# A state-space and feed-forward layer on one core: the same steps in another order on all five engines

## What is computed

```python
x = x + attn(layernorm(x))      # state-space layer, see below
x = x + ffn(layernorm(x))

def attn(u):
    zxbcdt = u @ W_in.T         # z0, x0 (512 each), xBC (544), dt (8 heads)
    dt = softplus(zxbcdt[..., -8:] + dt_bias);  A = -exp(A_log)
    xBC = silu(causal_conv4(xBC) + conv_b)      # x (8 heads x 64), B (16), C (16)
    h = exp(dt_t * A) * h + dt_t * x_t * B_t    # scanned over the rows
    y = h @ C_t + D * x_t
    y = layernorm(y) * ln_gamma + ln_beta
    y = sigmoid(y @ W_gate.T + b_gate) * y
    return concatenate([silu(z0) * x0, y]) @ W_out.T

def ffn(x):
    h = gelu(x @ ternary(W_fc).T)
    return layernorm(h, ln_w, ln_b) @ ternary(W_proj).T
```

## Time and profile before

| | us |
|---|---|
| median of 3 runs | 1097.28 |
| lowest and highest run | 1093.89, 1099.71 |
| span of the profiled execution, first to last instruction | 1095.2 |
| PE busy in it | 1049.7 (96%) |
| DVE busy | 966.7 (88%) |
| ACT busy | 962.1 (88%) |
| POOL busy | 496.6 (45%) |

### The profile page before, as it was taken

The page is one execution under the profiler, slowest core; times in us unless marked ns, Lnnn a source line. Parts: engine busy times, 40 slices in busy tenths (PEclk is TensorE's granted clock), DMA queues, the critical chain, the costliest instruction groups (busy, mean ns, idle before and its releaser), DMA issues.

```text
span 1095.2 us, 23188 instructions
## 1 busy us (share of the span) xinstructions
PE 1049.7 (96%) x8214; PEld 668.4 (61%) x8214; DVE 966.7 (88%) x2007; ACT 962.1 (88%) x1740; POOL 496.6 (45%) x590
## 2 busy tenths in 40 slices
PE   3877999999999999999999999999999999999997
PEld 1543756566575666657565665756666566666674
DVE  5998998999989999988999898899998988788766
ACT  5978698999999988899898999989899997989775
POOL 1543564353534544444434726443263733544552
PEclk9888999999999999999999999999999999999999
DMA  6702434245445265455336564353645433543668
GB/s 199 203 12 39 100 76 78 50 98 116 98 91 95 50 126 98 107 97 96 72 78 116 103 121 87 89 95 62 117 97 113 87 80 63 117 78 64 115 124 161
DMA packets 306708, 105.94 MB, mean 97 GB/s; under 512 B 275488, under 2 KB 302880, under 8 KB 306592
## 3 DMA queue, kind: packets, MB, share of 16 engines
q1 hardware_dynamic: 306592, 104.46, 47.7%
HBM read 24.32 MB, written 8.39 MB: 30 GB/s over the span
## 4 chain that ended last, share of the span: by engine, by line
PE 70%; DVE 11%; ACT 8%; issue 4%; DMA 3%; SPq 2%; POOL 1%; ACTq 0%; DVEq 0%; POOLq 0%
PE bank L399 44%; PE bank L634 8%; PE bank L622 7%; PE bank L560 3%; PE bank L569 2%; PE bank L475 2%; ACT L183 2%; DMA hT<-hb 2%; DVE cv L1018 2%; PE bank L521 1%; DVE EM L1138 1%; DVE st L981 1%; PE bank L545 1%; ACT EM L799 1%; DMA x<-in_x 1%
## 5 line engine op out<-in xcount | busy, mean ns | idle before, releaser
L399 PE MATMUL bank<-xnT,win 128*128 128x512 f16 (+1 forms) x1248 | 299.5, 387 | 19.6 <-DMA xnT<-hb 17.5
L399 PEld LDWEIGHTS bank<-xnT,win 128*128 128x128 f16 (+1 forms) x1248 | 122.2, 102 | 152.3 <-DVE win L930 17.5
L1018 DVE SCALAR_TENSOR_TENSOR cv<-bank,cws,cv 128x510 f32<-128x510 f32 (+5 forms) x240 | 177.4, 745 | 11.1 <-ACT tail L730 3.0
L399 PE MATMUL bank<-yhl,wg 128*128 128x512 f16 x768 | 173.0, 379 | 0.2
L1331 POOL TENSOR_TENSOR caty<-tg,caty 128x512 f16<-128x512 f32 x64 | 83.2, 1309 | 157.8 <-ACT caty L836 157.7
L183 ACT ACT_TABLE_LOAD x117 | 150.1, 1283 | 2.8 <-PEq L1526 0.7
L1326 POOL TENSOR_TENSOR yT<-yhl 128x512 f32<-128x512 f16 x64 | 79.6, 1265 | 113.8 <-DMA yhl<-ynh 113.8
L399 PEld LDWEIGHTS bank<-yhl,wg 128*128 128x128 f16 x768 | 74.3, 98 | 88.3 <-ACT EM L799 1.4
L1335 POOL TENSOR_TENSOR cat<-sz,cat 128x512 f16<-128x512 f32 x64 | 86.2, 1354 | 89.0 <-ACT cat L848 88.6
L634 PE MATMUL bank<-wpj,hT 128*128 128x256 f16 x1024 | 121.2, 273 | 5.2 <-DMA hT<-hb 5.2
L622 PE MATMUL bank<-wfc,x3T 128*128 128x512 f16 x512 | 122.2, 379 | 0.0
(11 more groups left out here) (154 smaller groups left out, 2048.4 us busy)
## 6 DMA issues: line engine op xcount, KB each, us to landing
x<-in_x SPq DMA_DIRECT2D x31, 512.0 KB, 3.8
out_y<-x SPq DMA_DIRECT2D x15, 512.0 KB, 2.9
crep<-cv SPq DMA_DIRECT2D x128, 32.0 KB, 2.0
hT<-hb SPq DMA_TRANSPOSE x128, 3.2
caty<-in_wg SPq DMA_DIRECT2D x1, 1024.0 KB, 7.2
x<-in_wout SPq DMA_DIRECT2D x1, 1024.0 KB, 6.7
hT<-in_wfc SPq DMA_DIRECT2D x1, 1024.0 KB, 6.1
hb<-in_wpj SPq DMA_DIRECT2D x1, 1024.0 KB, 8.4
```

What stands on the lines that cost most here:

```text
L399: m = eng.matmul(b, lhs(p, k), rhs(q, k), start=(n == 0), stop=(n == len(seq) - 1))
L1018: op = eng.scalar_tensor_tensor(cs[0:w, j, 3 - k:T], b[0:w, 0:T - 3 + k], cws[0:w, j, k:k + 1], cs[0:w, j, 3 - k:T], ALU.mult, ALU.add)
```

## The change

Only the five strings change. The words are the same ones, as letter and block, and as many of each (917 on PE, 1116 on ACT, 1108 on DVE, 439 on POOL, 334 on SP); they stand in another order, and the bank numbers on PE's words are assigned anew. The waits are made from the same code, so each names the same step as before, and PE's waits for a bank follow the new assignment. Table loads follow from ACT's order: the program of before has 117, that of after 108. The core of the diff, one line of PE's string:

```diff
 PE_ORDER = (
...
-    "G52 p34 v61 G56 r60532 q671 q646 w6 w6 f47 f41 p34 w6 w6 f46 f47 s70 f41 f45 y63 y66 y62 y64 x77 x71 p35 c83 "
...
+    "m71 v55 G57 G56 r65127 w6 w6 f44 v66 q653 f41 p30 w6 w6 f45 s73 c80 f44 x72 y61 f47 y65 f44 p36 y67 x72 p34 "
```

## The result

The changed kernel takes 1165.44 us (median of 4 runs, 1161.46 to 1167.61) against 1098.49 us for the kernel before on the same chip: ratio 1.0627, 95% interval 1.0604 to 1.0649. It is 67 us slower where 11.7 us were forecast. The sign was right; the size was wrong by more than five times, and the time lies far outside the range of 1098 to 1121 us. The profiled executions, from which all that follows is read, are 70.5 us apart (1165.7 against 1095.2 us).

The account below looks back on a forecast made before the run. PE's own queue was taken to bound nine tenths of the time. Order +13.4, start -0.7, ACT -1.0 and end 0 gave +11.7 us on the 1095.2 us span, 1106.9, plus 2.1 to the median: 1109.0 us, range 1098 to 1121.

Parts of the forecast that it names:

- PE's dearer order: Over PE's whole queue, mostly behind the start: the same matmuls in the new order take 13.4 us more, bounds 11 and 15.
- The +8.2 us: PE's whole queue: counting only changes of step kind, 260 before and 342 after, at 0.10 us each.
- entries, runs and lone steps: PE's queue: 43 more full-to-partial passages +4.3 us, 18 more `q` runs +5.8, parted `w` pairs +2.3, `q` off `r` +1.0.
- its cover: From 104 to 1050 us PE idles only 5.0 us, so no waiting there hides the added time.
- The start: First 104 us: a 1.2 us later input against about 1.9 us less DVE queue; net -0.7 us, range -6 to +4.
- The first product: Start of PE's work: expected at 18.7 us in place of 17.50, since ACT's moved cast delays the input's second half.
- ACT: Table loads fall from 117 to 108, ACT does 11.5 us less; effect on the time -1.0 us, bounds 0 and -5.
- The end: Last chunks' feed-forward chain: a `p` of block 14 nearer the end shortens nothing; 0 us, bounds -1 and +1.
- leave 90 us or more: From 104 to 1050 us: DVE and ACT were each said to have at least 90 us of idle time.
- The rival of new waits for `Y`: Between a block's last `w` and first `y`, PE waits for DVE: 6 to 25 us on top, 1115 to 1134 us; chance 0.16.
- all engines shift with PE: Argument against new waits for `Y`: the other engines' steps move along with PE's.
- Over 99% in the middle: Profile after the change: PE was still expected to be busy for over 99% of the middle stretch.

Follow-up runs that it names:

- before_split: The kernel before with only PE's order touched: 22 pairs of `q` and over 14 pairs of `w` parted by one step; 1112.1 us.
- after_hit: The changed kernel with the 107 of 196 wide POOL steps that lay over a lengthened DVE instruction narrowed to 8 columns; 1123.6 us.
- after_miss: The changed kernel with the other 89 of 196 wide POOL steps, over no lengthened DVE instruction, narrowed to 8 columns; 1154.7 us.
- before_first: The kernel before with the first steps of all five engines in the changed kernel's order, the rest in its own; 1129.7 us.
- after_first: The changed kernel with the first steps of all five engines in the order of the kernel before, the rest in its own; 1152.2 us.
- before_join_pieces: The kernel before with 18 PE steps moved next to their like and POOL's wide instructions cut into four pieces; 1146.2 us.

## Why the prediction was wrong in size

**PE's dearer order, +13.4 us: right.** 12.8 to 15.7 us by the price list, 14 to 15.6 us in before_split for a sequence priced at 11.4, 16.2 us between the two kernels with the other causes gone. The +8.2 us that the prediction counted by the rule on tiling modes of the Trainium skill (TensorEngine Tiling (Array Packing), section Tiling Modes) would have been too little. All of the counting of entries, runs and lone steps stands, and its cover was zero as said.

**The start, -0.7 us with bounds -6 and +4: wrong, +12.6 us.** The step that failed was costing it by DVE's queue ahead of one late point, the Gram masks of block 1. PE waits at three earlier links instead (4.42, 2.51 and 5.75 us), and nobody makes that up. Two of these links were priced, like all of DVE's, with durations of before, and were 2.1 and 2.5 us longer. The first product did not slip to 18.7 us either; it came at 17.71. The 1.2 us by which ACT's moved cast was to hold it up did not reach it.

**ACT, -1.0 us: the count was right, and it did not matter.** 108 loads as said, ACT 7.3 us less busy and not 11.5, and the kernel gained nothing from it: its exponential now waits 42.7 us in place of 20.4.

**The end, 0: +2.4 us**, outside its bound of 1 but small.

**The missing term, +42 us: the step that failed.** The prediction put PE's waits in the middle at nothing and had no line for them. Two things stand in its place. One says that DVE and ACT "leave 90 us or more" in the middle, and reads a mean as slack at each link. The other is an assumption that it does not state: every duration was carried over from before as if it were the instruction's own. In the earlier trace rows DVE has 966.7 us of busy time, and 32.5 us of that were already waits on POOL's instructions; a group like L1126, with a mean of 404 ns over a shortest of 341 and a median of 352, was the sign. An order of steps decides which instructions meet, and the new one makes 126 meet instead of 56. after_hit shows that this is the cause and after_miss that POOL's load is not. That the kernel would be slower was forecast for a reason that holds, but this reason carries a fifth to a quarter of the loss. That the other terms went the same way is luck. What the collisions cost PE depends on the room ahead of `r`: in the kernel before, 56 of them cost some 3 us, after the change 126 cost 42 to 44.

**The rival of new waits for `Y`** priced waits of the right kind, DVE coming late for a PE step, but at the wrong step: PE's `y` rows carry almost none, and `r` carries most. Its argument against itself, that "all engines shift with PE", was the weak one. DVE does not shift with PE when it is itself 91% busy (911.56 of 1004 us).

**"Over 99% in the middle"** fell at once: 969.20 of 1004 us is 96.5%.

## What to carry to other kernels

Before a new order is priced, compare each group's mean with its shortest instance. Here the difference was what the neighbour engine cost it, and the new order redrew it. Where DVE and POOL both work on SBUF, their meetings have to be scheduled like a bank, and a chain of short dependent DVE instructions (the state step, the dt step) was the worst place for one here. And a free 10% of an engine is no slack at a link where the next engine starts 0.15 us behind it, as PE's `r` did behind `S` in blocks 0, 2, 4 and 12.

## What the hardware showed that I had not expected

**A DVE instruction with all its operands in SBUF can stand until the wide POOL instruction in progress is over, and one that reads PSUM did not.** Over six of these traces (before, after, before_split, before_first, after_first, after_miss), of the DVE instructions that started with a wide POOL instruction (128 columns or more, over 1 us) in progress:

| DVE instruction | times | lengthened | mean lengthening, ns | mean rest of POOL's instruction, ns |
|---|---|---|---|---|
| `S<-S,dec,th` (SBUF only) | 73 | 69 | 675 | 873 |
| `tg<-tg,yT` (SBUF only) | 61 | 55 | 693 | 821 |
| `EM<-EM,Gm` (SBUF only) | 121 | 91 | 588 | 1064 |
| `dtv<-dtv,dtt`, 32 columns | 15 | 15 | 856 | 999 |
| `ahl<-dtt`, a cast with one input | 8 | 8 | 936 | 1077 |
| `cv<-bank,cws,cv` (PSUM) | 454 | 0 | 7 | 639 |
| `yT<-cv,small,bank` (PSUM) | 110 | 0 | 4 | 670 |
| `st<-x`, statistics of SBUF | 269 | 0 | 5 | 616 |

How near to the edges of POOL's instruction a meeting still counts moves these numbers of times by some 10%. Of the 30 `EM` that kept their length most met a POOL instruction that was itself longer than its like: there POOL was the one that stood.

The Trainium skill, SBUF — State Buffer, section SBUF: two separate sides, says that DVE and GpSimd share one pair of ports as an exclusive lock, which a DVE instruction needs in a two-port mode or with two SBUF inputs, and that whoever comes first keeps it for the whole instruction while the other blocks. The trace agrees in the main: for the short ones the lengthening is the rest of POOL's instruction less some 130 to 200 ns, cutting that instruction into four cut it to 0.23 us in the mean, the statistics with their one input were never held, and POOL's own instructions were lengthened by 108.3 us in the other direction. Two things go beyond it. POOL's `rs<-rs,mhalf` (a power over four columns, mostly 1.0 us) held nobody: of 142 DVE instructions of kinds that were held elsewhere and that began inside one, 139 kept their length, and the other three stood for the wide instruction behind it. And wide instructions without a pause between them can hold a DVE instruction one after the other, for 5.5 us in before_join_pieces. The rule would have asked for the count that the prediction lacks.

**Small instructions suffer most.** A product of 32 columns needs 0.19 us and took up to 1.16 us. The state step's four dependent instructions went from 1.50 us to as much as 4.02 us in one block.

**A wait costs twice on PE.** After a wait of 2.51 us the granted clock was 0.51 from 453.5 to 457 us, and the same `r` took 2.09 us in place of 1.17.
